# A two-layer adapter kernel: centroids folded in two steps, eight merges moved from the slots to the fold, deeper row buffers

## What is computed

```
# layer 0 (x: [128, 32, 512])
y     = (causal_conv(x, K) + D * x) * mask
base  = y @ base_w.T + base_b
delta = sum over the two best experts e of w_e * (y @ A.T) @ B[e].T
x1    = x + base + 0.5 * delta
# layer 1
c     = x1 @ cond_weight[adapter].T
dots  = softmax(c @ centroids.T / 0.1);   hits = dots > 0.01
dense = c @ weight.T + bias
out   = x1 + where(any hit in the row and in the column's cluster, dense, 0)
```

## Time and profile before

| what | value |
|---|---|
| median of three runs | 777.56 us |
| the profiled execution's own time | 782.75 us |
| its span, first to last instruction | 781.0 us |
| mean granted TensorE clock | 0.865 of full speed |
| PE, DVE, POOL, ACT busy | 84%, 58%, 55%, 23% |
| DMA | 142.6 MB, 183 GB/s in the mean |

### The profile page before, as it was taken

How to read it: one execution, slowest core, us unless ns; L and a number is a source line. 1 busy time by engine, 2 the same in 40 slices (tenths; PEclk the granted TensorE clock), 3 DMA queues, 4 the chain that set the end, 5 groups by cost and what they waited for, 6 DMA issues and landing times.

```text
span 781.0 us, 12108 instructions
## 1 busy us (share of the span) xinstructions
PE 653.2 (84%) x3496; PEld 549.3 (70%) x3497; DVE 451.7 (58%) x906; ACT 181.9 (23%) x340; POOL 427.0 (55%) x454
## 2 busy tenths in 40 slices
PE   0459999999995998999999746776878769999993
PEld 0349999999995998566665335665766648888882
DVE  6885666667667200566666313456455655666772
ACT  3112333332220000433332012222221211111110
POOL 4602265557666500355666633566666605788876
PEclk9969999999998555899999567868677869999997
DMA  6664656487950442466767456788978633444441
GB/s 188 134 197 139 203 151 174 148 264 235 261 151 19 161 151 52 140 220 216 221 219 253 172 175 207 280 282 264 296 244 287 222 104 108 143 153 148 149 134 40
DMA packets 98261, 142.60 MB, mean 183 GB/s; under 512 B 29224, under 2 KB 45966, under 8 KB 97186
## 3 DMA queue, kind: packets, MB, share of 16 engines
q1 hardware_dynamic: 82338, 100.59, 44.4%
q0 software_dynamic: 12992, 40.71, 13.7%
q10 hardware_dynamic: 2880, 0.67, 0.4%
HBM read 90.84 MB, written 52.93 MB: 184 GB/s over the span
## 4 chain that ended last, share of the span: by engine, by line
PE 60%; DVE 12%; POOL 10%; issue 8%; DMA 6%; SPq 1%; ACT 1%; POOLq 1%; ACTq 0%; DVEq 0%
PE acc L1715 14%; PE work L1669 8%; PE bcast L1760 7%; PE acc L1785 6%; PE bcast L1785 6%; POOL out_tile L864 5%; PE acc L1810 4%; PE acc L1808 4%; DMA two_rows<-expert_deltas_sorted 3%; PE acc L1900 2%; PE bcast L1852 2%; PE work L1655 2%; POOL out_row_of_tile L856 2%; PE work L1828 2%; DVE x1T_lo L1500 2%
## 5 line engine op out<-in xcount | busy, mean ns | idle before, releaser
L767 POOL TENSOR_TENSOR yT_lo<-y_masked,yT_hi 128x512 fp32r<-128x512 f32 x32 | 41.7, 1303 | 88.8 <-ACT yT_hi L922 88.3
L1030 ACT ACTIVATE x1T_hi<-work 128x512 fp32r<-128x512 f32 x78 | 46.5, 598 | 178.1 <-PE work L1828 175.5
L802 POOL DMA_INDIRECT gated_by_expert<-records,record_places x64 | 64.4, 1006 | 20.1 <-issue 16.2
L835 POOL DMA_INDIRECT expert_deltas_sorted<-x_group,records_of_slots x32 | 31.5, 984 | 72.4 <-DVE x_group L1467 64.8
L1500 DVE TENSOR_TENSOR x1T_lo<-work,x1T_hi 128x512 fp32r<-128x512 f32 x78 | 52.4, 682 | 27.7 <-ACT x1T_hi L1030 27.5
L1669 PE MATMUL work<-uT_hi,hankel 128*128 128x512 f32 (+3 forms) x256 | 66.3, 332 | 2.0 <-DMA hankel<-k_rev 2.0
L1467 DVE TENSOR_TENSOR x_group<-acc,base_b_bc 128x512 f32<-128x512 f32 x80 | 51.5, 682 | 6.7 <-PE acc L1810 4.0
L1852 PE MATMUL bcast<-merged_c,x1T_hi 128*128 x156 | 28.2, 308 | 27.3 <-DVE x1T_lo L1500 27.1
L1669 PEld LDWEIGHTS work<-uT_hi,hankel 128*128 128x128 f32 x256 | 46.9, 193 | 5.6 <-DVE uT_lo L1280 2.3
L864 POOL TENSOR_TENSOR out_tile<-dense_sel,cond_w 128x512 f32<-128x512 f32 x27 | 34.8, 1289 | 24.5 <-DVE dense_sel L1595 23.7
L835 POOL DMA_INDIRECT expert_deltas_sorted<-x_group,two_rows x36 | 35.4, 985 | 22.0 <-DVE x_group L1467 13.5
(11 more groups left out here) (319 smaller groups left out, 1571.5 us busy)
## 6 DMA issues: line engine op xcount, KB each, us to landing
hankel<-k_rev SPq DMA_DIRECT2D x32, 512.0 KB
two_rows<-expert_deltas_sorted SPq DMA_DIRECT2D x20, 512.0 KB, 4.7
x_rows<-x_base_sorted SPq DMA_DIRECT2D x39, 256.0 KB, 4.4
x_by_tile<-x_rows SPq DMA_DIRECT2D x39, 256.0 KB, 3.3
cond_w<-expert_deltas_sorted SPq DMA_DIRECT2D x19, 512.0 KB, 4.6
x_group<-in_x_dram SPq DMA_DIRECT2D x32, 256.0 KB, 4.4
cond_w<-in_L_cond_weight_dram SPq DMA_DIRECT2D x32, 256.0 KB
cond_w<-x_by_tile SPq DMA_DIRECT2D x27, 256.0 KB, 2.7
```

The source lines that it names most:

```text
L802: g.indirect_dma_start(rec_dram, bass.IndirectOffsetOnAxis(ap=place_u[gr % 2][:, m:m + 1], axis=0), both[:, m, :], None, bounds_check=last ...
L835: g.indirect_dma_start(d_dram, bass.IndirectOffsetOnAxis(ap=to_row, axis=0), dl[s % DL], None, bounds_check=last_d, oob_is_err=True).then_ ...
```

## The change

*Centroids in two steps.* `centroids(e)` now makes the transposed product: the stationary side is 64 columns of the centroids, the moving side 512 columns of the raw weight, four fp32 matmuls instead of 16, into 64 partitions of `bcast0`. ACT copies that to SBUF (`ctb`), and `centroids_back(e)` turns it with four fp32 matmuls against the identity (64 columns each) into `bcast1`, from where ACT and DVE take high and low parts as before.

*Fewer adapters in the joint.* Five (`MC_FIRST`) are done there; adapters 5, 6 and 7 come in batches 1, 4 and 7 (`MC_BATCH`): `centroids` ahead of the batch's experts, `centroids_back` behind them. Raw weights 4 to 7 have places of their own, 6 and 7 in memory that `mw` fills later.

*Merges.* `MERGE_BATCH` names eight batches. The fold has 24 merges: three ahead of the tiles, 17 in the triples (two in triples 2, 5, 8 and 11), four after the last tile (`[NT] * 4`).

*Buffers in the fold.* `XR` 6 and `DR` 4; the added ones lie where the last four merges write, so these wait for the end of the fold.

*Layout of the deltas.* A delta row lies at `2 * row + q`, so both deltas of a row are 4 KB in one piece, and one DMA descriptor reads both.

*Semaphores.* Some are merged to make room (`d_ev` is one counter instead of four; three small loads share one).

The core of the diff:

```diff
@@ -40,8 +40,8 @@
...
 PAIRS = NT // 3
-XR = 4
-DR = 2
+XR = 6
+DR = 4
@@ -63,9 +63,12 @@
...
 ORDER = (4, 5, 6, 7, 0, 1, 2, 3)
-MERGE_BATCH = list(range(16))
+MERGE_BATCH = [2, 3, 5, 6, 8, 9, 12, 14]
 NM2 = len(MERGE_BATCH)
-MERGE_TILE = [-1] * 3 + [3 * p for p in range(PAIRS)]
+MC_FIRST = 5
+MC_BATCH = {1: 5, 4: 6, 7: 7}
+RAW_SEM = (0, 1, 2, 3, 0, 2, 3, 2)
+MERGE_TILE = [-1] * 3 + [3 * p for p in range(PAIRS) for _ in range(1 + (p in (2, 5, 8, 11)))] + [NT] * 4
@@ -273,11 +282,12 @@
...
         raws.close()
-        raw = [w_id, raw_a, raw_b, raw_late]
+        raw = [w_id[:, :, :], raw_a[:, :, :], raw_b[:, :, :], raw_late[:, :, :], w_id[:, :, :], raw_a[:, :, :]]
+        raw += [mw_f32[1][:, e, :, :] for e in (6, 7)]
...
         w_sp = [[alloc(fold, f"cond_w_{m}_{n}", [P, LB, P], F32R) for m in ("hi", "lo")] for n in range(2)]
-        x_ring = alloc(fold, "x1_rows", [P, XR, L])
+        x_ring = alloc(fold, "x1_rows", [P, LB, L])
@@ -300,8 +310,9 @@
...
         w_blk = [w_flat[:, L * n:L * n + L].rearrange("p (a k) -> p a k", a=LB) for n in range(2)]
-        xr = [x_ring[:, n, :] for n in range(XR)]
-        dr = [rows2[:, :, :], w_id[:, 2:4, :]]
+        last = ORDER[-1]
+        xr = [x_ring[:, n, :] for n in range(LB)] + [mw_f32[0][:, last, n, :] for n in range(2)]
+        dr = [rows2[:, :, :], w_id[:, 2:4, :]] + [mw_f32[1][:, last, 2 * n:2 * n + 2, :] for n in range(2)]
@@ -471,7 +481,16 @@
...
             turn = MERGE_TURN[m - 4]
-            return 0 if turn in (None, -1) else turn + 3
+            return 0 if turn in (None, -1) else min(turn + 3, NT - 1)
+
+        def block_batch(m):
+            return PTS - 1 if m < 4 else MERGE_BATCH[m - 4] + 5
+
+        def merges_before(b):
+            return sum(x < b for x in MERGE_BATCH)
+
+        def mc_before(b):
+            return MC_FIRST + sum(x < b for x in MC_BATCH)
@@ -575,10 +594,20 @@
...
             sp.wait_ge(pr_ps, len(PREP))
-            sp.dma_start(raw[0][:, :, :], cw[0, :, :, :]).then_inc(s_raw[0], 16)
-            for e in range(4, IDS):
-                sp.wait_ge(mc_ps, e - 3)
-                sp.dma_start(raw[e % 4][:, :, :], cw[e, :, :, :]).then_inc(s_raw[e % 4], 16)
+            sp.dma_start(raw[0], cw[0, :, :, :]).then_inc(s_raw[0], 16)
+            def load_raw(e):
+
+                sp.dma_start(raw[e], cw[e, :, :, :]).then_inc(s_raw[RAW_SEM[e]], 16)
+
+            for e in (4, 5):
+                sp.wait_ge(ct_mm, e - 3)
+                load_raw(e)
+            sp.wait_ge(b_done, H)
+            sp.wait_ge(ct_mm, 3)
+            sp.wait_ge(x1_st[2], 16 * len(range(2, NG, XB)))
+            load_raw(6)
+            sp.wait_ge(g_rdy, NG)
+            load_raw(7)
@@ -618,24 +647,28 @@
...
 
-                sp.dma_start(dr[t % DR], d_parts[bass.ds(part, 1), :, :, :].rearrange("t p q l -> (t p) q l")
+                sp.dma_start(dr[t % DR].rearrange("p q l -> p (q l)"), d_parts[bass.ds(part, 1), :, :]
+                             .rearrange("t p l -> (t p) l")
...
                 sp.wait_ge(x1_st[n], 16 * len(range(n, NG, XB)))
-            parts = [load_base(t) for t in range(XR - 1)]
+            parts = [load_base(t) for t in range(3)]
...
             for t in range(DR):
+                if t >= 3:
+                    parts.append(load_base(t))
                 load_deltas(t, parts[t])
-            sp.dma_start(onehot.bitcast(I32), bass.AP(assignments.tensor, 0, [[0, C], [1, L]])).then_inc(s_asg, 16)
+            parts.append(load_base(DR))
+            sp.dma_start(onehot.bitcast(I32), bass.AP(assignments.tensor, 0, [[0, C], [1, L]])).then_inc(s_db, 16)
...
                 if t + XR - 1 < NT:
-                    if t:
+                    if t >= 1:
@@ -969,19 +1002,17 @@
...
 
+                act.wait_ge(ct_mm, e + 1)
+                if e >= 2:
+                    act.wait_ge(mc_ps, e - 1)
+                a.activation(ctb[e % 2], bb[0][0:C, :], ACT.Copy).then_inc(ct_ev, 1)
                 act.wait_ge(mc_ps, e + 1)
-                if e == 0:
-                    for n in range(2):
-                        act.wait_ge(s_rec[n], 16 * GH * NQ * (NG // 2 - 1))
-                if e == 5:
-                    for n in range(2):
-                        act.wait_ge(s_rec[n], 16 * GH * NQ * NG // 2)
-                a.activation(mc[:, e, :, 0:C], bb[e % 2][:, 0:LB * C].rearrange("p (k c) -> p k c", k=LB), ACT.Copy
+                a.activation(mc[:, e, :, 0:C], bb[1][:, 0:LB * C].rearrange("p (k c) -> p k c", k=LB), ACT.Copy
...
 
-                act.wait_ge(s_raw[m % 2], 16 * (m // 2 + 1 + IDS // 4))
+                act.wait_ge(s_raw[m % 2], 16 * (m // 2 + 1 + RAW_SEM.count(m % 2)))
@@ -990,6 +1021,10 @@
...
                 e, k = merged(m)
+                if m == NMERGE - LB:
+                    act.wait_ge(xd_ps, NT)
+                    for n in range(LB, XR):
+                        act.wait_ge(s_xst[n], stores_of(n, XR))
@@ -1018,6 +1053,8 @@
...
                     split_high(m + 2)
+                if b in MC_BATCH:
+                    centroids_high(MC_BATCH[b])
@@ -1249,7 +1286,7 @@
...
                 v.tensor_scalar(sort_row[:, :], g_iota, place[:, 5:6], None, ALU.add).then_inc(t_rdy, 1)
-                chain.after(v.tensor_scalar(place[:, 7:8], place[:, 0:1], float(H), None, ALU.mult))
+                chain.after(v.tensor_scalar(place[:, 7:8], place[:, 0:1], float(H * NQ), None, ALU.mult))
@@ -1489,6 +1528,8 @@
...
                     merged_low(MERGE_BATCH.index(b))
+                if b in MC_BATCH:
+                    centroids_low(MC_BATCH[b])
@@ -1748,17 +1789,27 @@
...
 
-            def centroids(e):
-
-                pe.wait_ge(s_raw[e % 4], 16 * (e // 4 + 1))
-                if e == 0:
+            def centroids(e, waits=0):
+
+                pe.wait_ge(s_raw[RAW_SEM[e]], 16 * (1 + RAW_SEM[:e].count(RAW_SEM[e])))
+                if e:
+                    pe.wait_ge(ct_ev, e)
+                else:
                     pe.wait_ge(pr_hi, len(PREP))
-                if e >= 2:
-                    pe.wait_ge(mc_ev, e - 1)
+                if waits:
+                    pe.wait_ge(m_lo, waits)
+                for o in range(LB):
+                    last = mm(bb[0][0:C, :], f_c[:, o, :], raw[e][:, o, :], start=(o == 0), stop=(o == LB - 1))
+                last.then_inc(ct_mm, 1)
+
+            def centroids_back(e):
+
+                pe.wait_ge(ct_ev, e + 1)
+                if e:
+                    pe.wait_ge(mc_ev, e)
                 for k in range(LB):
-                    for o in range(LB):
-                        last = mm(bb[e % 2][:, C * k:C * k + C], raw[e % 4][:, o, P * k:P * k + P], f_c[:, o, :],
-                                  start=(o == 0), stop=(o == LB - 1))
+                    last = mm(bb[1][:, C * k:C * k + C], ctb[e % 2][:, P * k:P * k + P], ident[0:C, 0:C],
+                              start=True, stop=True)
@@ -1769,14 +1820,19 @@
...
 
-            for e in range(IDS):
+            for e in range(MC_FIRST):
                 centroids(e)
+                if e:
+                    centroids_back(e - 1)
...
                     slot_rows()
-
-            def merge(m):
+            centroids_back(MC_FIRST - 1)
+
+            def merge(m, waits=0):
...
                 pe.wait_ge(cw_lo, m + 1)
+                if waits:
+                    pe.wait_ge(mc_ev, waits)
@@ -1817,10 +1873,12 @@
...
                 if b in MERGE_BATCH:
-                    if b == MERGE_BATCH[0]:
-                        pe.wait_ge(mc_ev, IDS)
-                    merge(MERGE_BATCH.index(b))
+                    merge(MERGE_BATCH.index(b), mc_before(b))
+                if b in MC_BATCH:
+                    centroids(MC_BATCH[b], merges_before(b))
                 experts(b)
+                if b in MC_BATCH:
+                    centroids_back(MC_BATCH[b])
```

63 lines of the change are left out of this document (35 added, 28 removed).

## The result

The change made the kernel faster by more than was forecast: 743.06 us in the median of four runs (742.25 to 746.17) against 776.74 for the kernel before, ratio 0.957 with a 95% interval of 0.953 to 0.962. Two later comparisons gave 0.966 (0.957 to 0.976) and 0.950 (0.946 to 0.954). Forecast was 756.5 (744 to 778): right in its sign, but the time lies just under the range.

The account below looks back on a forecast made before the run. It took PE to bound the joint at its lower clock, PE or POOL the slots, and PE the fold. Terms 24.6 + 6 − 4 − 5.5 = 21.1 us, taken from 777.56, gave 756.5 us, range 744 to 778.

Parts of the forecast that it names:

- the 6 us for the rings: Beginning of the fold: more row and delta buffers cut PE's waits for POOL; gain 6 us, bounds 0 to 14.
- the −4 for the double triples: Fold: second merges in four triples mostly fill PE's wait for DVE; loss 1 us each, 4 in all.
- Joint: Centroids stage: transposed matmuls run at the higher clock; first expert at 292.6 instead of 319.35, gain 26.8 us.
- Rival A: Joint: clock stays at the lower level in the long fp32 matmuls, slower than before; 797 us, chance 0.08.
- Slots: Expert batches: end at 423.6 instead of 448.2, POOL bounding the late ones; 24.6 of the 26.8 us gained are left.
- Tail: End of the fold: four merges after the last dots; dense stage starts 18 us after them instead of 10.9; −5.5 net.
- the give-back of 1.6: First dense product after the tail: warm clock gives back 1.6 us (4.5 against 2.74).
- D: Rival: fold faster, with a clock held up by the second merges; 10 us less, 746 us, chance 0.08.
- B: Rival: moved merges are paid in full in the fold; 25.5 us more, 782 us, half of it 769; chance 0.07.
- C: Rival: POOL or the clock in the late slots; 11 batches cost 12.5 us more, 769 us, chance 0.12.

Follow-up runs that it names:

- merges_12: The changed kernel with twelve merges between slots and none doubled in the fold: 762.3 us, ratio 0.978 to the kernel before.
- The filler: Twelve useless matmuls of 512 columns in each of 13 triples, added to the changed kernel with twelve merges between slots, none doubled: 748.9 us, ratio 0.953.
- second and third group: Two of four sets of kernels measured together; the changed kernel again took 758.7 us in one, with useless matmuls in nine single triples 753.3 in the other.
- single_late: The changed kernel with a single triple's one merge moved between the last transpose and the last dots: 772.9 us, ratio 0.984 to the kernel before.

## Why the prediction was right and where it failed

Two terms of the sum failed, both in the fold: the 6 us for the rings, which priced one engine's wait at the beginning instead of the pace of every tile, and the −4 for the double triples, which left out what a wait of PE costs in clock. Together they stood for 2 us, and the fold gave 24.4.

**Joint: right, by its own steps.** That the transposed product lifts the clock rested on the earlier trace rows, and the clock is 0.93. The terms above were within about 0.3 us. The first expert came within 0.4, partly by luck: the last copy ended 1.1 early (at 284.1 instead of 285.2), and the way from there to the first expert took 8.2 instead of 7.4. Rival A, which would have been slower than before, had the busy PE at 0.50 for it; it falls with calls of 3.62 instead of 7.09 us. The Trainium skill ("TensorE: Matmul & The Clock Gate", Part 1: The HAM clock gate) speaks of how busy PE is alone; here the less busy of the two by the profile, 26.09 of 30.50 us against 56.01 of 56.50, has the higher clock. The length of the moving side doesn't settle it either: the experts at the end of the slots have 512 moving columns each, PE is busy all the time, and the clock is 0.50:

```profile
409.10:420.70 11.60, 11.60 (x16) 4.57 (x16) 6.67 (x11) 1.09 (x2) 8.86 (x10) 0.50 0.53 206
```

**Slots: right.** 23.1 us left of 27.1, against 24.6 of 26.8. POOL's pace was that of the earlier trace rows but for one gap of 4.57 us between its stores at 379.65 and 384.22, 3.3 more than 1.29: a batch without a merge had run at the lower level (6.5 us from the transposes at 370.37 to those at 376.85, where the sum had POOL's 5.16), and the merge behind it began there too.

**Fold, beginning: the step failed in scope.** I took 6 of the 14.0 us that PE waited for POOL, and so sized the rings by the wait of one engine in one place. What they set is the pace of every tile. A delta buffer of the kernel before is freed by POOL's sum, loaded again by SP and used two tiles later. POOL's sums and SP's issues of that loop in the kernel before:

```profile
510.60 1.28 POOL L846 TENSOR_TENSOR x_rows<-x_rows,cond_w 128x512 f32<-128x512 f32 x1 [1.09 <-DMA cond_w<-expert_deltas_sorted]
511.95 1.27 POOL L848 TENSOR_TENSOR x_rows<-x_rows,cond_w 128x512 f32<-128x512 f32 x1
...
518.24 1.58 POOL L846 TENSOR_TENSOR x_rows<-x_rows,cond_w 128x512 f32<-128x512 f32 x1
...
527.55 1.28 POOL L846 TENSOR_TENSOR x_rows<-x_rows,cond_w 128x512 f32<-128x512 f32 x1 [2.19 <-DMA cond_w<-expert_deltas_sorted]
```

```profile
513.70 0.39 SPq L621 DMA_DIRECT2D cond_w<-expert_deltas_sorted  x1
...
521.73 0.39 SPq L621 DMA_DIRECT2D cond_w<-expert_deltas_sorted  x1
```

The sums that use the buffer `cond_w` end at 513.22, the load is issued at 513.70, and the next sum from that buffer begins at 518.24, 7.6 us after the one at 510.60; the round after takes 9.3 us, with a wait at its end. Two tiles in 7.6 and 9.3 us are 3.8 to 4.7 a tile, 11.5 to 14 a triple, just about the 12.55 of PE. So two loops of about the same length ran side by side. An estimate from the trace of before alone gives it: (0.5 to issue + 4.7 to land, the median of its loads + 2.6 of sums) / 2 buffers × 3 tiles = 11.7.

**Fold, double triples: the wrong sign.** I put −1 each, −4 in all, with a gain of 2 each as the bound, "clock higher afterwards". The measured gain lies beyond that bound: with deep rings the four second merges bring 11.9 us, 3 each. A double triple is indeed the longer one, by 1.8; what was left out is that the single ones get shorter, 10.0 in the mean, and all eight take 10.7 instead of the 11.9 of merges_12. The term that failed is the price of a wait on PE. In merges_12 PE waits 2.7 us in the mean (1.9 to 3.7) ahead of a triple's last dots. Behind that come mostly a merge at the lower level (4.5 against 2.74 by the prediction's rows) and transposes and dots at the lower level too (1.11 against 0.66 for four transposes). The filler shows it. With twelve merges between slots and filler, eight triples lie between the transposes at 502.03 and 579.25, 9.7 us each; without filler six lie between 469.57 and 540.72, 11.9 each. Not every wait is followed by the lower level: in the changed kernel 1.80 us before 561.20 was (the next merge's first four matmuls took 2.06), and 1.92 before 552.28 wasn't (1.19). With shallow rings the same second merges cost 14.8, so the −4 stood between two answers, and the rings decided which one.

**Tail: right in size** (18.1 against 18), but the give-back of 1.6 didn't come: the first dense product still takes 2.07 us; the level had fallen again.

**The rivals.** D, the faster fold with a clock held by second merges, named the clock half of the mechanism and not the rings. Its 746 meets the time within 3 us by luck, for it had 10 us more in the fold where the traces have 22.4. It had 0.08, for I took it as an extra and not as what follows if the loads no longer bind. B did not occur in this kernel; a cost of its size (14.8) is seen where the delta rings stay small. C is seen in small in this trace (the gap of 4.57 us above) and in full in the second and third group, where the slots take 13 to 14 us more.

The two effects don't add up. Against the 178.7 us of before, the fold is 12.6 us shorter with the rings alone, 15.5 longer with the doubled merges alone, and 24.5 shorter with both. Added to the other terms, this would have given 734, 9 below the median, of which 3.3 are the other stages and 5.6 the dear profile.

## What to carry to other kernels

Estimate the pace of a ring of buffers as (issue + landing + use) / depth, here 3.9 us a tile beside PE's 4.2, for every ring, and compare it with the stage's period even where no engine seems to wait for it. Where two loops stand at the same height, edit both or expect nothing, and cost the edits together. A wait of PE can cost more than its length, by the lower clock after it. Work that fills the wait can be free, even useless work, provided that its outputs don't queue ahead of what PE needs next (single_late).

## What was not expected of the hardware

- Useless matmuls made a kernel faster: 156 of them took 23 us off a fold of 166.1, 108 of them with two earlier loads 12 us off the changed kernel.
- The slots of the changed kernel ended at 437.9 in one group and at 425.1 and 421.5 elsewhere, with the first expert within 1.3 us and the fold within 1.5; both the longest and the shortest have chip number 5. The cause is open.
- PE was busy for 11.60 of 11.60 us with matmuls of 512 moving columns, and the clock stayed at 0.50.
- Reading a delta row in one piece of 4 KB instead of two of 2 KB changed nothing: 741.0 us with two pieces.
